# Score products of the two 16-head attentions as 32-row tiles of 256 columns, over one score buffer of four banks

## The reference

```
# block 2: queries from the normed x, keys and values from the context
q = rope(LN(x) @ wq.T + bq); k = rope(ctx @ wk.T + bk); v = ctx @ wv.T + bv
attn = softmax(einsum('bqhd,bkhd->bhqk', q, k) / sqrt(8))
x = x + tanh(g) * (einsum('bhqk,bkhd->bqhd', attn, v) @ wo.T + bo)

# block 3: no projections; keys and values are the context itself; masked keys
energy = einsum('nqhd,nkhd->nhqk', LN(x), ctx); energy = where(mask == 0, -1e20, energy)
x = x + tanh(g) * (einsum('nhqk,nkhd->nqhd', softmax(energy / sqrt(128)), ctx) @ Wo.T + bo)
```

## Time and profile before

| | |
|---|---|
| median of 3 runs | 2138.75 us (2138.2 to 2139.11) |
| profiled execution, its own time | 2140.66 us |
| its span, first to last instruction | 2138.6 us |
| PE busy | 1921.8 us, 90% of the span |
| DVE busy | 1553.0 us, 73% |
| ACT, POOL busy | 821.7 us, 744.8 us |
| mean granted TensorE clock | 0.936 of full speed |

### The profile page before, as it was taken

One profiled execution on the slowest core, in us unless ns is written; L12 is line 12 of the kernel. 1 busy time (PEld: TensorE's weight loads), 2 busy tenths in 40 slices (PEclk: granted clock), 3 DMA queues, 4 the chain that ended last, 5 costly groups with the idle time before them and its releaser, 6 DMA issues. The chain is left out here.

```text
span 2138.6 us, 41675 instructions
## 1 busy us (share of the span) xinstructions
PE 1921.8 (90%) x14275; PEld 1028.0 (48%) x14275; DVE 1553.0 (73%) x3177; ACT 821.7 (38%) x1492; POOL 744.8 (35%) x981
## 2 busy tenths in 40 slices
PE   5659998999999988999999998979998999989975
PEld 2544444444444444555555554435664444436641
DVE  4767877878778776777777775757785666768978
ACT  3632012012011114666666663325662222225655
POOL 4551112112112014776676664455640000022222
PEclk8559999999999999999999999998997999999975
DMA  4312132032032032000000000000002524221001
GB/s 114 123 46 61 36 65 60 21 78 60 20 80 60 20 84 102 2 2 1 0 0 0 0 2 1 1 7 15 14 8 63 142 67 121 62 63 19 16 1 40
DMA packets 60079, 89.66 MB, mean 42 GB/s; under 512 B 23720, under 2 KB 42024, under 8 KB 55472
## 3 DMA queue, kind: packets, MB, share of 16 engines
q1 hardware_dynamic: 59952, 88.04, 16.7%
HBM read 80.85 MB, written 2.97 MB: 39 GB/s over the span
## 5 line engine op out<-in xcount | busy, mean ns | idle before, releaser
L952 POOL TENSOR_TENSOR l0f_v<-l0f_val,l0f_top 64x256 f32<-64x256 f32 x128 | 78.4, 613 | 484.8 <-DVE l0f_val L1230 477.3
L1059 PE MATMUL l0f_acc<-l0f_z,w_all 128*128 128x512 f32 x512 | 228.8, 609 | 15.0 <-DVE l0f_z L1268 15.0
L1008 PE MATMUL l0f_work<-w_all,l0f_xs 128*128 128x512 f32 x384 | 183.4, 600 | 15.1 <-DVE l0f_val L1225 14.4
L1059 PEld LDWEIGHTS l0f_acc<-l0f_z,w_all 128*128 128x128 f32 x512 | 99.2, 195 | 143.9 <-issue 123.6
L255 POOL TENSOR_SCALAR var_eps<-mean_var 128x4 f32<-128x4 f32 (+1 forms) x64 | 14.7, 229 | 377.6 <-DVE mean_var L239 375.5
L1474 PE MATMUL l1x_proj_v<-l1x_wvo,l1x_cs 128*64 128x512 f32 x512 | 136.0, 610 | 0.0
L1230 DVE COPY_PREDICATED l0f_val<-l0f_oh,l0f_work 128x512 f32<-128x512 int32 x160 | 116.7, 729 | 22.8 <-PE l0f_work L1008 7.9
L2876 ACT ACTIVATE l2f_act_g<-l2f_pg 128x512 f32<-128x512 f32 x104 | 61.5, 594 | 146.2 <-PE l2f_pu L2811 130.4
L2819 PE MATMUL l2f_acc<-l2f_hid,w_all 128*128 128x512 f32 x208 | 107.6, 599 | 9.6 <-DVE l2f_hid L2957 9.6
L2951 DVE TENSOR_TENSOR l2f_hu<-l2f_act_g,l2f_pu 128x512 f32<-128x512 f32 x104 | 71.1, 684 | 61.9 <-ACT l2f_act_g L2876 60.3
L2810 PE MATMUL l2f_pg<-xnT_all,w_all 128*128 128x512 f32 x208 | 109.3, 608 | 0.0
(11 more groups left out here) (399 smaller groups left out, 4425.1 us busy)
## 6 DMA issues: line engine op xcount, KB each, us to landing
l0f_first_mask<-onehots SPq DMA_DIRECT2D x32, 512.0 KB, 5.7
w_all<-onehots SPq DMA_DIRECT2D x32, 512.0 KB, 11.7
w_all<-combination SPq DMA_DIRECT2D x40, 256.0 KB, 5.0
w_all<-in_weights SPq DMA_DIRECT2D x1, 4640.0 KB, 16.8
l0x_m_b<-running_max SPq DMA_DIRECT2D x16, 256.0 KB, 4.6
w_all<-combination SPq DMA_DIRECT2D x16, 224.0 KB, 4.3
w_all<-combination SPq DMA_DIRECT2D x16, 192.0 KB, 4.1
w_all<-combination SPq DMA_DIRECT2D x16, 160.0 KB, 4.2
```

Source lines behind the costliest of these rows:

```text
L952: nc.gpsimd.tensor_tensor(v2[a * SEQ:(a + 1) * SEQ, t % 2, b, :, :], val[r, t % 2, :, :].rearrange("p (c a) k -> p c a k", a=2)[:, :, a, : ...
L1008: nc.tensor.matmul(value_banks[e % 3][:, :], xs[:, t * P:(t + 1) * P], ve[:, e, :], start=True, stop=True).then_inc(ve_done, 1)
L1059: nc.tensor.matmul(acc[:, :], oe[:, n % E, n // E, :], z[:, n % Z, :], start=(n == 0), stop=(n == C * E - 1)).then_inc(acc_done, 1)
```

## The change

The array is cut into row strips of 32 instead of 64. A tile's scores become eight products of 32 rows (four heads), 64 weight columns and 256 moving columns, and each strip r has a bank of its own, of which the first 256 columns are used. There is one buffer of four banks instead of two of two; the PSUM that it takes is the same. The wait before the scores of tile m is now for m subtractions. The mask is written by four products of 256 columns. DVE reads the scores through a pattern with one more dimension (`by_row`). `km` has four slots to a head instead of eight, so it is 4096 columns instead of 8192, and the memset with it. `first_bank`, which names the eight banks for the first projections of a4, names the same banks.

```diff
-        eng.dma_start(km[r, half, :, :, h % 8, :].rearrange("p t b k -> p (t b) k"),
+        eng.dma_start(km[r, half, :, :, h % 4, :].rearrange("p t b k -> p (t b) k"),
...
-        score = [ps(f"score{i}", (P, 1024)) for i in range(2)]
+        score = ps("score", (P, 2048))
+        R, HR = 4, H // 4
+        score_bank = [score[:, r * 512:(r + 1) * 512] for r in range(R)]
+        by_row = score[:, :].rearrange("p (r n) -> p r n", r=R)[:, :, 0:HR * SEQ].rearrange("p r (h k) -> p r h k", h=HR)
...
                 def mask(m, u, half, t):
-                    after(pe, sub_done, m - 1)
+                    after(pe, sub_done, m)
...
-                        for a in range(2):
-                            nc.tensor.matmul(score[t % 2][:, a * 512:(a + 1) * 512], core.ident_bf[:, :],
-                                             bcast(mask_bf[:, bass.ds(m, 1), :].rearrange("p one k -> p (one k)"), 1, C),
+                        for r in range(R):
+                            nc.tensor.matmul(score_bank[r][:, 0:HR * SEQ], core.ident_bf[:, :],
+                                             bcast(mask_bf[:, bass.ds(m, 1), :].rearrange("p one k -> p (one k)"), 1, HR),
                                              start=True, stop=False, skip_group_check=True)
 
                 def scores(t, half):
                     for b in range(2):
-                        for a in range(2):
-                            ins = nc.tensor.matmul(score[t % 2][b * SEQ:(b + 1) * SEQ, a * 512:(a + 1) * 512],
-                                                   qT[a * 64:(a + 1) * 64, half, t * P + b * SEQ:t * P + (b + 1) * SEQ],
-                                                   km[a * 64:(a + 1) * 64, half, t, b, :, :].rearrange("p a k -> p (a k)"),
+                        for r in range(R):
+                            rows = slice(r * 32, (r + 1) * 32)
+                            ins = nc.tensor.matmul(score_bank[r][b * SEQ:(b + 1) * SEQ, 0:HR * SEQ],
+                                                   qT[rows, half, t * P + b * SEQ:t * P + (b + 1) * SEQ],
+                                                   km[rows, half, t, b, :, :].rearrange("p h k -> p (h k)"),
                                                    start=own, stop=True, skip_group_check=True)
                     ins.then_inc(score_done, 1)
...
-                    nc.vector.tensor_reduce(mx[:, t % 2, :], score[t % 2][:, :].rearrange("p (h k) -> p h k", h=H),
-                                            AX.X, ALU.max).then_inc(max_done, 1)
+                    nc.vector.tensor_reduce(mx[:, t % 2, :].rearrange("p (r h) -> p r h", r=R), by_row, AX.X, ALU.max)\
+                        .then_inc(max_done, 1)
...
-                    nc.vector.tensor_tensor(diff[:, :, :], score[t % 2][:, :].rearrange("p (h k) -> p h k", h=H),
-                                            bcast(mx[:, t % 2, :], 2, SEQ), ALU.subtract).then_inc(sub_done, 1)
+                    nc.vector.tensor_tensor(diff[:, :, :].rearrange("p (r h) k -> p r h k", r=R), by_row,
+                                            bcast(mx[:, t % 2, :].rearrange("p (r h) -> p r h", r=R), 3, SEQ),
+                                            ALU.subtract).then_inc(sub_done, 1)
...
-            km = core.sb(late, "keys_by_head", [P, 2, G, 2, 8, SEQ])
+            km = core.sb(late, "keys_by_head", [P, 2, G, 2, 4, SEQ])
```

More of the change, by code:

```diff
@@ L2183, in narrow_attention @@
         o_turned, oT_ready, y_done, res_done = sem("o_turned"), sem("oT_ready"), sem("y_done"), sem("res_done")
-        first_bank = lambda u, i, kind: (misc[:, :], score[0][:, 0:512], score[0][:, 512:1024], score[1][:, 0:512],
-                                         score[1][:, 512:1024], pT[:, :], po[0][:, :], po[1][:, :])[4 * u + 2 * kind + i]
+        first_bank = lambda u, i, kind: (misc[:, :], score_bank[0], score_bank[1], score_bank[2],
+                                         score_bank[3], pT[:, :], po[0][:, :], po[1][:, :])[4 * u + 2 * kind + i]
         if own:
```

## The result

The changed kernel takes 2161.95 us (median of 4 runs, 2159.88 to 2167.8); the kernel before, on the same chip, 2138.47 us (2137.45 to 2139.11). The ratio is 1.0115 (95% interval [1.0094, 1.0135]): 23 us slower, where 2.6 were forecast. The profiled execution of the changed kernel took 2160.88 us, its span is 2158.9.

What follows compares the result with a forecast made beforehand. It took a4 to go round through PE, DVE and POOL, and a6 to be paced by DVE. Terms -0.7 + 0.8 + 1.9 + 0.6 = +2.6 us on the median 2138.75 gave 2141.3 us; 8-in-10 range 2133.5 to 2148.5.

Steps and rivals of the forecast that it cites:

- The product: Score products in both stages: 0.40 us shorter, 0.62 us to PE's next instruction, 0.76 us to the maximum.
- two and two: Score products: lower bound of the gain, nothing, if the strips run two by two; upper bound 0.43 us.
- the rival of the sequencer: Score products: about 62 ns per matmul, 16 records 0.99 us, no gain; same end as products not overlapping four-fold, chance 0.1.
- The DVE patterns and the memset: Patterns between -0 and +0.05 us each, nearest 0; `km` memset halves, 6.93 to 3.5 us, covered.
- The lost buffer in a4: Fourth product of an a4 group waits for the subtraction; gain 0.12 us a group, six groups -0.7, bounds +0.6 and -5.4.
- So the end comes only one operation earlier, 0.26 us: a4 normalisation: one operation slips between two of POOL's, the second waits; subtraction ends 1514.50, transpose 1515.18 instead of 1515.30.
- the normalisation gets ahead of POOL: Rival, faster: DVE asks 0.36 us earlier in a4, which gains 0.9 a group, -5.4; 2135.0, down to 2131; chance 0.25.
- The rival's sum: Normalisation ahead of POOL: -5.4 + 0.8 + 0.9 + 0 at the starts, at their lower ends, = -3.7, 2135.0.
- The clock: Rival, slower: PE idles 2 to 3 us more at both starts, half clock adds +2 to +4, 2145; chance 0.17.
- The start of each stage: First tiles wait for one another's subtraction: a6 +1.9, bounds +0.7 and +3.5; a4 +0.6, bounds 0 and +2.
- the credit for the half-clock time: Stage starts: part of PE's earlier half-clock time falls into the wait, reducing +3.0 in a6 and +2.0 in a4.
- Forecast +0.8: Steady part of a6: DVE waits 0.20 us once a group, +1.4 for seven groups, partly given back; bounds 0 and +1.5.

Runs made afterwards that it cites:

- e4: Changed kernel plus two products whose results nobody reads, ahead of the fourth product of a group of a4, in five groups; 2154.65 us, 1.0066.
- e6: Changed kernel with POOL's `a_qT` addition in a4 waiting until the four operations of DVE's normalisation are done; 2146.37 us, 1.0042.
- e7: Kernel before, with POOL's `a_qT` addition in a4 waiting until DVE's normalisation is done; 2132.12 us, 0.998.
- e9: e6 plus products whose results nobody reads, where PE waits in the first three tiles of both stages; 2136.8 us, 0.9997.
- e5: Changed kernel with the waits for queries and keys put ahead of the wait for the subtraction; 2164.7 us, 1.0132.
- e1: Kernel before, with 64-row products and two buffers kept, but scores waiting as if there were one buffer; 2164.67 us, 1.0119.

## Why the prediction was wrong

*The product: right.* 0.69 us for 16 records, 0.62 to the next instruction, 0.79 to the maximum (0.76 forecast). The sum that let all eight products run together came out, two and two were no bound, and the rival of the sequencer is refuted: a record comes every 0.69 / 16 = 43 ns at most. The DVE patterns and the memset cost what was said, 1.21 to 1.22 us and 3.51 us.

*The lost buffer in a4: the step that failed.* "So the end comes only one operation earlier, 0.26 us" holds POOL's next rotation where it was. I moved PE's product by 0.40 us, followed it to the residual and the normalisation, and did not follow the other thing that it releases: PE's key projection, ACT's copy `w_all`, POOL's next rotation. Counted from the start of the same product, ACT ends that copy 2.94 us later before (1509.32 to 1512.26) and 2.57 after (1510.47 to 1513.04). In the earlier trace rows POOL's addition ends at 1511.52, and its next rotation starts 0.9 us later; in that pause the last three operations of DVE passed. I had taken the pause for given, and it shrank to 0.17 us. Of that, 0.36 is the slip that I had counted: POOL's addition starts 1.29 us behind the product instead of 0.93. The other 0.37 is the earlier copy, and it decided: DVE's fourth operation came at 1513.29, 0.09 us behind the rotation, which by these rows would have started at 1513.57 with the copy where it was. At the stage's first normalisation the slip and the earlier copy are there too, but the rotation starts 0.46 us behind the copy instead of 0.16 (the trace doesn't show why), the pause is 0.50 us, and the fourth operation passes:

```profile
1489.94 2.09 DVE L247 TENSOR_SCALAR xn<-x_all,mean_var,rstd 128x128 f32 x4
...
1491.94 2.49 POOL L2255 TENSOR_TENSOR w_all<-w_all,consts 128x512 f32<-128x512 f32 x2 [0.50 <-ACT w_all L2547]
```

The forecast of -0.7 us came out at +16: about 6 by the late normalisation (net of the shorter product), about 10 by the clock (e4). The rival "the normalisation gets ahead of POOL" was right about which race decides, and e6 shows its price when the race is forced: six groups of 117.0 us, 4.5 under before against the 5.4 worked out. 4.0 of them come without the change (e7). In the kernel after the race was lost, not won. The rival's sum also takes 0.9 us for the starts at their lower ends, where the bounds given are 0.7 and 0; that moves it by 0.2 us.

*The clock: right kind, wrong place and size.* I looked for it at the starts alone and gave it 2 to 4 us. It fell in five of the six groups, where the wait at the fourth product was 1.4, 2.4, 3.7, 2.4 and 2.5 us, not 1 to 1.5. PE was still busy 119.8 of 137.5 us there. The wait itself holds one small misreading: 0.06 us from subtraction to PE was read in a6 and used in a4, where the kernel before has about 0.15 (subtraction ended at 1445.20, product at 1445.34), as has the kernel after.

*The start of each stage.* a4 +2.3 (forecast +0.6, bounds 0 and 2), a6 +4.5 (forecast +1.9, bounds 0.7 and 3.5), both above their bounds. The chain of waits was right, transposes of tile 0 later by 2.3 us in a4 (2.0 forecast). In a6 they came 4.9 us later, not 3.0: mask and scores of tiles 1 and 2 were counted at full clock, 1.29 us to the maximum, and ran at half, 2.23 us (1933.45 to 1935.68), which is 1.9 us for the two. What was also wrong is the credit for the half-clock time "which now falls into the wait". PE stayed at half clock longer: 0.50 through all of a4's start, now 19.0 us, and 0.61 for 0.76 in a6's. e9 gets 3.3 and 1.7 us of it back by keeping PE busy.

*a6.* Forecast +0.8, found +4.3 for six groups. 2.4 of it are the first group (19.7 for 17.3), at half clock until 1955.4, the rest 0.4 us a group: 0.34 us instead of 0.06 between subtraction and mask, read at a place outside the loop, of which e5 explains 0.09. DVE's wait is 0.47 us where I had 0.20. e1 (17.9) and the kernel after (17.3) show the gain of the shorter product in a6 as 0.6 us a group, and the single buffer as more than that.

*The range.* Its far ends stood for one failed step each. Here one step, the race with POOL, lengthened the wait at which the clock fell, in four of the five groups with half clock, and both then added up. In the fifth (PE's wait at 1494.57) the single buffer's own wait of 1.42 us was enough.

## What to carry to other kernels

When an edit moves an instruction earlier, follow each thing that it releases, on every queue, and not only the one toward the end of the stage: a few tenths of a microsecond can let a third engine into a stretch that had been free by chance. A race between two engines that is decided by such a margin is better fixed by a wait (e7: 3.6 us for one wait) before anything near it is tuned. If a second buffer must go, look at what the writer does while it waits for the reader: a wait of TensorE can cost its clock as well as itself, and work of no use in that place can be cheaper than none (e4, e9).

## What the runs showed of the hardware

- Sixteen fp32 records of 32x64 tiles, four row strips by two column strips with 256 columns, pass in 0.69 us at full clock, 1.16 at half; eight of 64x64 with 512 columns in 1.09. The gain was 0.40 us a tile.
- VectorE's `tensor_scalar` and GpSimd's `tensor_tensor` took turns by single operations. Four VectorE operations that take 1.11 us alone took 2.11, 3.16 and 4.35 us with one, two and three GpSimd operations between them. VectorE's maximum and subtraction of scores in PSUM ran beside them at their usual 1.21 and 1.22 us.
- TensorE's granted clock fell to half in most groups of a stage where PE was busy 87% of the time and waited 1.4 to 3.7 us once a group. In e1, with waits of 1.1 us in four groups and 2.1 in one, it was at half for 3.4 us of the same stage against 31.7, and the 2.1 us were not where it fell. A wait of 1.43 us was followed by half clock in e6 and not in e9. Two products of no use in the wait gave about 10 us back.
- From the end of the subtraction to PE's first instruction behind its wait lie, in a6, where PE waits for one thing, 0.06 us in the groups written out one by one and 0.14 in the loop; where it waits for three, 0.34 in the loop (0.25 with the late one put last). In a4, which has no mask, it is 0.15 us wherever PE waits for one thing, in the loop or not.
